# FFN1's down product with its rows in two float32r parts in place of three bf16 parts

## The reference

```
def _quantized_matmul(x, w, scale):
    wq = w.astype(jnp.float8_e4m3fn).astype(x.dtype)
    y = jnp.einsum('bsi,io->bso', x, wq)
    return y * scale
gate = jax.nn.silu(_quantized_matmul(x, gate_w, gate_scale))
up = _quantized_matmul(x, up_w, up_scale)
fuse = gate * up
return _quantized_matmul(fuse, down_w, down_scale)
```

## Time and profile before

| | |
|---|---|
| median of 3 runs | 433.9 us |
| the runs | 435.48, 429.26, 433.9 us |
| profiled execution | 434.21 us |
| its span | 432.5 us |
| PE busy | 399.0 us (92%) |
| VectorE busy | 294.8 us (68%) |
| ScalarE busy | 234.5 us (54%) |
| GpSimd busy | 184.5 us (43%) |
| DMA over the span | 22.98 MB, mean 53 GB/s |

### The profile page before, as it was taken

One profiled execution on the slowest core, in us unless ns is written; L12 is line 12 of the kernel. 1 busy time (PEld: TensorE's weight loads), 2 busy tenths in 40 slices (PEclk: granted clock), 3 DMA queues, 4 the chain that ended last, 5 costly groups with the idle time before them and its releaser, 6 DMA issues.

```text
span 432.5 us, 14682 instructions
## 1 busy us (share of the span) xinstructions
PE 399.0 (92%) x6376; PEld 234.9 (54%) x6376; DVE 294.8 (68%) x572; ACT 234.5 (54%) x377; POOL 184.5 (43%) x291
## 2 busy tenths in 40 slices
PE   5799889999999988999799998899999999879997
PEld 5356664555556336544477465553555553465476
DVE  4645589999998106741336587999999960288883
ACT  3635356577786973332101643565786779545950
POOL 5107013336153444569594000336263446363870
PEclk9989899999999999999899999999999999999999
DMA  6799541000000000010200578300000000000002
GB/s 204 126 253 281 120 127 28 5 3 3 5 2 5 5 2 6 21 53 2 73 0 2 155 190 213 107 5 4 3 4 4 3 5 4 2 0 2 1 26 73
DMA packets 21662, 22.98 MB, mean 53 GB/s; under 512 B 2592, under 2 KB 20862, under 8 KB 21598
## 3 DMA queue, kind: packets, MB, share of 16 engines
q1 hardware_dynamic: 20502, 19.03, 17.5%
q0 software_dynamic: 544, 2.49, 2.0%
q10 hardware_dynamic: 552, 0.53, 0.4%
HBM read 8.27 MB, written 1.05 MB: 22 GB/s over the span
## 4 chain that ended last, share of the span: by engine, by line
PE 62%; DVE 15%; POOL 6%; ACT 6%; DMA 6%; issue 3%; SPq 2%; DVEq 0%; ACTq 0%; POOLq 0%
PE ps L842 11%; DVE mx L1320 11%; PE ps L822 11%; PE ps L800 10%; PE ps L1072 5%; ACT prob L1201 5%; PE ps L1004 5%; PE ps L979 4%; PE ps L1040 4%; PE ps L734 3%; DMA col_rows<-in_L_ffn_up_scale 3%; PE ps L902 2%; PE ps L808 2%; POOL oT L561 1%; DMA oT<-in_L_ffn_gate_w 1%
## 5 line engine op out<-in xcount | busy, mean ns | idle before, releaser
L1320 DVE TENSOR_REDUCE mx<-ps 128x1 f32<-128x512 f32 (+3 forms) x304 | 180.7, 656 | 23.3 <-PE ps L808 18.3
L1201 ACT ACTIVATE prob<-ps 128x1024 f32<-128x1024 f32 (+1 forms) x192 | 145.6, 812 | 64.7 <-PE ps L822 64.5
L800 PE MATMUL ps<-kS,qS 99*32 99x512 bf16 (+21 forms) x1536 | 111.2, 318 | 5.2 <-DVE mx L1320 3.3
L822 PE MATMUL ps<-qS,kS 101*32 101x512 bf16 (+7 forms) x1536 | 96.0, 326 | 4.7 <-ACT prob L1201 3.8
L618 POOL TENSOR_SCALAR_AFFINE_SELECT prob<-prob 128x256 f32<-128x256 f32 x128 | 51.9, 412 | 109.0 <-ACT prob L1201 107.7
L842 PE MATMUL ps<-prob,v 128*32 128x512 f32 (+3 forms) x768 | 80.5, 489 | 0.7 <-POOL prob L618 0.5
L800 PEld LDWEIGHTS ps<-kS,qS 99*32 99x32 bf16 (+1 forms) x1536 | 42.9, 95 | 46.3 <-DVE mx L1320 22.9
L822 PEld LDWEIGHTS ps<-qS,kS 101*32 101x32 bf16 (+1 forms) x1536 | 36.4, 96 | 33.7 <-ACT prob L1201 17.2
L805 PE MATMUL ps<-mask_q,identb 128*32 128x32 bf16 (+1 forms) x1024 | 49.3, 184 | 2.0 <-issue 2.0
L808 PE MATMUL ps<-mask_q,identb 128*32 128x64 bf16 (+1 forms) x512 | 44.4, 196 | 0.0
L805 PEld LDWEIGHTS ps<-mask_q,identb 128*32 128x32 bf16 x1024 | 28.2, 97 | 14.6 <-issue 10.6
(11 more groups left out here) (149 smaller groups left out, 546.0 us busy)
## 6 DMA issues: line engine op xcount, KB each, us to landing
qS<-parts SPq DMA_DIRECT2D x24, 128.0 KB, 3.1
kS<-parts SPq DMA_DIRECT2D x24, 128.0 KB, 2.8
qS<-prob SPq DMA_DIRECT2D x12, 128.0 KB, 6.7
kS<-prob SPq DMA_DIRECT2D x12, 128.0 KB, 6.6
qS<-xn SPq DMA_DIRECT2D x12, 128.0 KB
kS<-xn SPq DMA_DIRECT2D x12, 128.0 KB
out<-x SPq DMA_DIRECT2D x8, 128.0 KB, 1.7
oT<-in_L_ffn_gate_w POOLq DMA_DIRECT2D x1, 768.0 KB, 4.9
```

Source lines behind the costliest of these rows:

```text
L800: mmi = nc.tensor.matmul(span[r:r + STRIP, 0:seen], qS[0:K_MAX[L], c, g * G + h, qt * P + r:qt * P + r + STRIP], kS[0:K_MAX[L], g * G + h, ...
L822: mmi = nc.tensor.matmul(bank[r:r + STRIP, off:CH], kS[0:K_EXP[L], h, kt * P + r:kt * P + r + STRIP], qS[0:K_EXP[L], c, h, off:CH], start= ...
L1201: nc.scalar.activation(prob[:, n % 3, 2 * pair:2 * pair + 2, off:CH], ps[:, 2 * (m % 2):2 * (m % 2) + 2, off:CH], ACT.Exp, scale=SCALE).th ...
L1320: ins = nc.vector.tensor_reduce(mx[:, slot, qt, heads[0]:heads[-1] + 1, part], src, AX_X, ALU.max)
```

## The change

`f3`, three bf16 parts, becomes `f2`, two parts in float32r, TensorE's 4-byte format with a shortened mantissa: the writer rounds to it. The first part is ScalarE's rounding of the whole, the second is the whole minus the first, written by VectorE in the same format (`hidden_lo`, in the place of `hidden_left`). ScalarE's `hidden_mid`, GpSimd's loop of 12 subtractions and the semaphores `f_left` and `f_mid` go. `d1` becomes float32r as well, so GpSimd's last step of `round_down` writes 4-byte values. The down product has 2 x 6 = 12 products per tile, 96 in all, where there were 144. `qS`, `kS` and `w0` are now allocated ahead of all other tiles, in scopes that end, so that `f2` and `d1` can be placed over them with a type of their own.

```
-        f3 = [q_flat[:, n * HT * T:(n + 1) * HT * T].rearrange("p (k t) -> p k t", k=HT) for n in range(2)] + [kS[:, 0:HT]]
+        f2 = sb("f2", [P, 2, NH * T // 2], F32R)[:, :, 0:HT * T].rearrange("p s (k t) -> p s k t", k=HT)
-        d1 = w0[:, :, :, :].rearrange("p m j i -> p (m j i)").bitcast(BF16)[:, 0:HT * C].rearrange("p (k i) -> p k i", k=HT)
+        d1 = sb("d1", [P, 4 * CJ * C], F32R)[:, 0:HT * C].rearrange("p (k i) -> p k i", k=HT)
...
 (GpSimd, at its end)
-            for n in range(NC * HT):
-                span = hidden_span(n)
-                pool.wait_ge(f_left, n + 1)
-                pool.wait_ge(f_mid, n + 1)
-                nc.gpsimd.tensor_tensor(f3[2][:, n % HT, span], f_rest[:, n % 3], f3[1][:, n % HT, span], ALU.subtract).then_inc(f_lo, 1)
...
 (TensorE, products_down1)
-                    for s, done in enumerate((f_hi, f_mid, f_lo)):
+                    for s, done in enumerate((f_hi, f_lo)):
                         pe.wait_ge(done, (FFN_C.index(t // TPC) + 1) * HT)
                         for ht in range(HT):
-                            mmi = nc.tensor.matmul(bank[:, 0:C], f3[s][:, ht, t * P:(t + 1) * P], d1[:, ht, :],
-                                                   start=s + ht == 0, stop=s == 2 and ht == HT - 1)
+                            mmi = nc.tensor.matmul(bank[:, 0:C], f2[:, s, ht, t * P:(t + 1) * P], d1[:, ht, :],
+                                                   start=s + ht == 0, stop=s == 1 and ht == HT - 1)
...
 (ScalarE)
-                        nc.scalar.copy(f3[0][:, n % HT, hidden_span(n)], f_whole[:, n % 3]).then_inc(f_hi, 1)
-
-                def hidden_mid(n):
-                    if n >= 0:
-                        act.wait_ge(f_left, n + 1)
-                        nc.scalar.copy(f3[1][:, n % HT, hidden_span(n)], f_rest[:, n % 3]).then_inc(f_mid, 1)
+                        nc.scalar.copy(f2[:, 0, n % HT, hidden_span(n)], f_whole[:, n % 3]).then_inc(f_hi, 1)
...
 (VectorE)
-                def hidden_left(n):
+                def hidden_lo(n):
                     if n >= 0:
                         dve.wait_ge(f_hi, n + 1)
-                        if n >= 3:
-                            dve.wait_ge(f_lo, n - 2)
-                        nc.vector.tensor_tensor(f_rest[:, n % 3], f_whole[:, n % 3], f3[0][:, n % HT, hidden_span(n)],
-                                                ALU.subtract).then_inc(f_left, 1)
+                        nc.vector.tensor_tensor(f2[:, 1, n % HT, hidden_span(n)], f_whole[:, n % 3],
+                                                f2[:, 0, n % HT, hidden_span(n)].bitcast(F32), ALU.subtract).then_inc(f_lo, 1)
```

More of the change, by code:

```diff
@@ L53 @@
 F32, BF16, FP16, I32 = mybir.dt.float32, mybir.dt.bfloat16, mybir.dt.float16, mybir.dt.int32
+F32R = mybir.dt.float32r
 ALU = mybir.AluOpType
@@ L310, in sem @@
             return ctx.enter_context(nc.semaphore(name))
+        with ExitStack() as scores:
+            qS = scores.enter_context(nc.sbuf_tensor("qS", [P, NC, NH, CH], BF16))
+            kS = scores.enter_context(nc.sbuf_tensor("kS", [P, NH, T], BF16))
+        f2 = sb("f2", [P, 2, NH * T // 2], F32R)[:, :, 0:HT * T].rearrange("p s (k t) -> p s k t", k=HT)
+        with ExitStack() as early:
+            w0 = early.enter_context(nc.sbuf_tensor("w0", [P, 4, CJ, C], F32))
+        d1 = sb("d1", [P, 4 * CJ * C], F32R)[:, 0:HT * C].rearrange("p (k i) -> p k i", k=HT)
         ps = ctx.enter_context(nc.psum_tensor("ps", [P, 8, CH], F32))
@@ L319, in two_layer_kernel @@
         rest = sb("rest", [P, 2, CH], F32)
-        qS = sb("qS", [P, NC, NH, CH], BF16)
-        kS = sb("kS", [P, NH, T], BF16)
         v1 = sb("v1", [P, NT, NH, 2 * HD], F32)
@@ L330, in two_layer_kernel @@
         mT = sb("mT", [2 * G * TPC, 2, P], BF16)
-        w0 = sb("w0", [P, 4, CJ, C], F32)
         w1r = oT[:, :, :].rearrange("p g t -> p (g t)")[:, 0:4 * CJ * C].rearrange(
@@ L387, in two_layer_kernel @@
         fT = q_flat.bitcast(F32)[:, 0:HT * T].rearrange("p (k t) -> p k t", k=HT)
-        f3 = [q_flat[:, n * HT * T:(n + 1) * HT * T].rearrange("p (k t) -> p k t", k=HT) for n in range(2)] + [kS[:, 0:HT]]
-        f_whole, f_rest = prob[:, :, 0], prob[:, :, 1]
+        f_whole = prob[:, :, 0]
         y = prob[:, :, 2, 0:C]
@@ L432, in two_layer_kernel @@
         fx_hi = sem("fx_hi")
-        f_hi, f_left, f_mid, f_lo = sem("f_hi"), sem("f_left"), sem("f_mid"), sem("f_lo")
+        f_hi, f_lo = sem("f_hi"), sem("f_lo")
         y_done = sem("y_done")
@@ L1251, in _ @@
                             hidden_hi(i * HT + ht - 1)
-                            hidden_mid(i * HT + ht - 2)
                 if L == 0:
@@ L1259, in _ @@
                     hidden_hi(NC * HT - 1)
-                    hidden_mid(NC * HT - 2)
-                    hidden_mid(NC * HT - 1)
         @block.vector
@@ L1446, in _ @@
                                 dve.wait_ge(f_hi, k1 - 2)
-                                dve.wait_ge(f_left, k1 - 2)
+                                dve.wait_ge(f_lo, k1 - 2)
                             ins = nc.vector.scalar_tensor_tensor(f_whole[:, k1 % 3], bank, s1[:, 1, ht:ht + 1], sg[:, n % 2],
@@ L1453, in _ @@
                         if L == 1:
-                            hidden_left(k1 - 1)
+                            hidden_lo(k1 - 1)
                 if L == 0:
@@ L1463, in _ @@
                 else:
-                    hidden_left(NC * HT - 1)
+                    hidden_lo(NC * HT - 1)
                 for n, t in enumerate(DOWN_ORDER[L]):
```

## The result

| | before | after |
|---|---|---|
| median, 20 runs each | 431.86 us | 428.3 us |
| lowest and highest | 429.16 to 435.48 | 422.84 to 431.44 |
| ratio | | 0.9881, 95% interval 0.9848 to 0.9913 |
| profiled execution, span | 434.21, 432.5 | 425.40, 423.6 |

The ratio leaves out runs that lie over 1.5% above the fastest of their kernel, which takes out eight of the changed kernel's 20, at mean clocks of 0.988 and 0.991, and, by the lowest and highest times above, none of before's, so it leans towards the change. It says -5.1 us, with -3.8 and -6.6 as its ends; the medians of all runs differ by 3.6. The change is faster, by less than the 2% that I took as the line.

What follows compares the result with a forecast made beforehand. PE's products were taken to bound the last down stage: 48 fewer give -5.24 us, all other terms 0, so 428.7 us from a median of 433.9. Range 424 to 435.5, the forecast's own 424.0 to 430.2.

Steps and rivals of the forecast that it cites:

- What bounds the stage: FFN1's down stage: PE busy 15.72 of 15.73 us, so the stage lasts as long as its 144 products, 109 ns each.
- 48 products go, 5.24 us: FFN1's down product: 48 products fewer at 109.2 ns each take 5.24 us off the chain, the most this edit can give.
- 96 products change their format, taken at 109 ns, 10.5 us: Remaining down products in float32r: bounded by 10.5 and 41.5 us, low end taken, 4-byte weight loads hiding as in transposes.
- Sum -5.24, 428.7 us: Whole kernel: -5.24 + 0 = -5.2 us, 428.7 us by the median of the runs shown, 1.2% faster.
- Second half in time, banks, VectorE: Fifth down tile: inputs 2.0 us early, PSUM bank 1.1 us early, VectorE level with PE by then; costed at nothing.
- Copies and subtractions, GpSimd's 4-byte d1, addresses: 0: ScalarE's 12 copies and GpSimd's 12 subtractions gone, d1 written as 4-byte values, SBUF addresses moved: each costed at 0.
- Half pace: Rival, down product: 4-byte moving columns pass every second cycle, 20.7 us, +5.0, 438.9 us; chance 0.10.
- float32's pace: Rival, down product: float32r runs like float32, 432 ns a product, 41.5 us, +25.7, 459.6 us; chance 0.04.
- Loads not hidden: Rival, down product: 4-byte weight loads stand 92 ns longer between products, 201 ns each, +3.6, 437.5 us; chance 0.04.
- The gain given back: Rival, down stage: second half's parts, PSUM banks or stores come late, between 429 and no change, 434; chance 0.06.

## Why the prediction was right, and where it was off

- *What bounds the stage.* Right. PE was the chain before and after, and with 144 float32r products the total moved by the difference of the products, within its interval.
- *48 products go, 5.24 us.* Right in mechanism and size: fp16 gives all of it.
- *96 products change their format, taken at 109 ns, 10.5 us.* The side was right (one load, one sweep a product, a quarter of float32's 432), the size was not: 120 ns, 11.51 us. This is the term that was mis-sized, by 1.02 us. The failing step is the choice of row for the load. I had 190 ns of a float32 product and 141 of a transpose and called the transposes the closest, because they leave the same room. The load is the product's, 192 ns. The transposes' columns also move at half rate, so that room was not the same use of PE either.
- *Sum -5.24, 428.7 us.* Measured 428.3. By the chain the gain is 4.22; the interval around the ratio's -5.1 has both in it. That the median met the forecast so closely is luck, as its errors offset each other: the median of before was 431.86 over 20 runs, not 433.9 over 3, so the forecast started 2.0 us too high, took off 1.0 too much, and the measured median lies 0.7 above the 427.6 that 4.2 us less would give.
- *Second half in time, banks, VectorE.* Right: no idle PE. VectorE caught up at the third tile, not the fifth, since its two last subtractions ended 2.2 us after the first down product and not 3.2; and its additions to x took 0.42 us each. Before, the two that ran beside GpSimd's last subtractions took 0.93 and 0.92, the six behind them 0.42 or 0.43; now GpSimd is idle. The first of them:

```profile
418.12 0.93 DVE L1478 TENSOR_TENSOR x<-prob,x 128x256 f32<-128x256 f32 x1
```

- *Copies and subtractions, GpSimd's 4-byte d1, addresses: 0.* Right as far as the runs show. The first by the chain and by the kernel with 144 products, the second by its row below, 1002 ns as with bf16, the third as far as the stages above show.

```profile
L570 POOL TENSOR_TENSOR d<-parts x4: 1000/1002/1004, 298.9 to 355.5; 128x384 fp32r<-128x384 f32 x4
```

- *Rivals.* Half pace and float32's pace are ruled out: 120 ns a product. Loads not hidden, the case of the Trainium skill's rule on row groups ("TensorE: Matmul & The Clock Gate", Part 3, "The mechanism"), would be 201 ns; the loads overlap though all use the same rows. But 11 of those 92 ns did appear, and I had priced this rival as all or nothing. The gain given back: no.

## What to carry to other kernels

When a dense run of products is the end of the chain, the number of products times their pace is the whole account; cutting a part pays even where other engines lose nothing. Before going from bf16 to a wider format for fewer parts, try fp16 where the values' range allows it: its 2-byte weight loads hide fully where float32r's cost 11 ns of 120 (128x128 weights, 256 moving columns). No run here tells how the precision of the two compares. To compare profiles of a kernel with a clock that drops at other places each run, compare stages of equal clock, not spans.

## What the runs showed that I had not expected

- A float32r product of 128x128 weights and 256 columns starts every 120 ns, one of 512 columns every 227, one of 128 columns every 111; fp16 has 109, 216 (FFN1's gate and up products) and 56. So going from 256 to 128 moving columns halves fp16's time and takes 9 ns off float32r's.
- fp16 weight loads take 98 ns for 128 columns but 124 for 96: the full width loads faster than a narrower one.
- The clock's lower level, 1.2 GHz, comes in stretches whose number differs from run to run: besides the one at the very end, before's profile has three, the changed kernel's one. The places recur: ten of the twelve profiles have one in FFN0's down stage, the changed kernel's first does not. There it costs 24.11 - 22.43 = 1.7 us, two fifths of what this change is worth.
